# Eight-batch macaron block on one core: the slot-table scatters of the attention stage are issued elsewhere in GpSimd's program

## The reference, cut to what matters

```
x = x + 0.5 * ffn(layernorm(x))      # 8 experts, 2 per token, fixed capacity
x = x + attn(layernorm(x))           # 16 heads, rotary positions, decay mask, no softmax
x = x + 0.5 * ffn(layernorm(x))
```

## Time and profile before

| | us |
|---|---|
| median of 3 runs | 2408.15 |
| the runs | 2403.44, 2408.15, 2408.89 |
| the profiled execution: its own time | 2403.44 |
| its span | 2401.6 |
| PE busy | 2187.6 |
| DVE busy | 1341.5 |
| POOL busy | 1163.4 |
| ACT busy | 1008.5 |

### The profile page before, as it was taken

The page is one execution under the profiler, slowest core; times in us unless marked ns, Lnnn a source line. Parts: engine busy times, 40 slices in busy tenths (PEclk is TensorE's granted clock), DMA queues, the critical chain, the costliest instruction groups (busy, mean ns, idle before and its releaser), DMA issues.

```text
span 2401.6 us, 57464 instructions
## 1 busy us (share of the span) xinstructions
PE 2187.6 (91%) x22468; PEld 1914.7 (80%) x22468; DVE 1341.5 (56%) x3312; ACT 1008.5 (42%) x2149; POOL 1163.4 (48%) x911
## 2 busy tenths in 40 slices
PE   6749999999999996999999999739999999999997
PEld 6738888999999995777777777628888899999997
DVE  7744444555555552577778877645444455555552
ACT  4433334444444441445555555423333343444442
POOL 4754777444444443222244444364776544444443
PEclk9999999999999998999999999859999999999998
DMA  8522433444434334112111211132443434343432
GB/s 331 200 91 48 82 91 84 104 79 98 81 96 92 89 77 98 37 38 73 58 55 57 73 57 74 56 120 49 82 90 78 84 98 84 94 99 82 100 80 29
DMA packets 129221, 209.40 MB, mean 87 GB/s; under 512 B 24876, under 2 KB 105328, under 8 KB 122864
## 3 DMA queue, kind: packets, MB, share of 16 engines
q0 software_dynamic: 57344, 69.21, 17.5%
q1 hardware_dynamic: 71696, 137.62, 16.6%
HBM read 136.03 MB, written 72.88 MB: 87 GB/s over the span
## 4 chain that ended last, share of the span: by engine, by line
PE 50%; DVE 4%; issue 3%; ACT 1%; POOL 1%; another core or an unknown queue 1%; DMA 1%; POOLq 0%; DVEq 0%; ACTq 0%
PE bank L632 15%; PE bank L643 15%; PE bank L716 10%; PE bank L804 3%; PE bank L837 1%; PE bank L772 1%; PE bank L621 1%; PE bank L787 1%; PE bank L822 1%; PE bank L876 1%; PE bank L734 1%; POOL slot_table L381 0%; DVE aw L1756 0%; DVE xnl L1730 0%
## 5 line engine op out<-in xcount | busy, mean ns | idle before, releaser
L1098 ACT ACTIVATE h<-bank 128x512 f32<-128x512 f32 x512 | 307.3, 600 | 923.7 <-PE bank L632 787.2
L1665 DVE CAST hh<-h 128x512 fp32r<-128x512 f32 x512 | 223.9, 437 | 763.6 <-ACT h L1098 683.3
L643 PE MATMUL bank<-w2h,hh 128*128 128x256 f32 x2048 | 585.2, 286 | 5.6 <-issue 5.5
L643 PE MATMUL bank<-w2h,hl 128*128 128x256 f32 x2048 | 582.4, 284 | 4.0 <-issue 3.8
L643 PE MATMUL bank<-w2l,hh 128*128 128x256 f32 x2048 | 582.2, 284 | 4.0 <-issue 3.8
L632 PE MATMUL bank<-xh,w1h 128*128 128x512 f32 x1024 | 411.1, 401 | 12.9 <-issue 6.0
L643 PEld LDWEIGHTS bank<-w2h,hh 128*128 128x128 f32 x2048 | 393.4, 192 | 26.0 <-issue 6.8
L418 POOL DMA_INDIRECT xe<-xn_rows,tab x256 | 272.4, 1064 | 290.7 <-issue 259.8
L643 PEld LDWEIGHTS bank<-w2l,hh 128*128 128x128 f32 x2048 | 393.8, 192 | 23.2 <-issue 6.1
L632 PE MATMUL bank<-xl,w1h 128*128 128x512 f32 x1024 | 408.7, 399 | 1.8 <-issue 1.8
L632 PE MATMUL bank<-xh,w1l 128*128 128x512 f32 x1024 | 402.8, 393 | 1.3 <-issue 1.3
(11 more groups left out here) (209 smaller groups left out, 3312.1 us busy)
## 6 DMA issues: line engine op xcount, KB each, us to landing
stg<-in_L_ffn_w SPq DMA_DIRECT2D x64, 1024.0 KB
xb<-acc SPq DMA_DIRECT2D x9, 1024.0 KB, 8.0
xa<-in_L_attn_x SPq DMA_DIRECT2D x8, 1024.0 KB, 14.0
xn_rows<-xa SPq DMA_DIRECT2D x8, 1024.0 KB
xn_rows<-xn_r SPq DMA_DIRECT2D x8, 1024.0 KB
xr<-acc SPq DMA_DIRECT2D x7, 1024.0 KB
out_rows<-xr SPq DMA_DIRECT2D x7, 1024.0 KB
slot_table<-pay,idx POOLq DMA_INDIRECT x256
```

Source lines behind the costliest of these rows:

```text
L643: last = pe.matmul(o, a[:, fj, s], c[:, fj, :], start=(fj == 0 and n == 0 and t % 2 == 0), stop=(fj == FJ - 1 and n == 2), skip_group_chec ...
L1098: act.activation(h32[fj % 2][:], bank[fj % 2][:], ACT.Gelu_apprx_tanh).then_inc(f.gelu, 1)
L1665: dve.tensor_copy(hh[:, fj, :], h32[fj % 2][:]).then_inc(f.hh, 1)
```

## The change

In POOL's `sequence(b)` the three calls `slots(b - 3, 1)`, `slots(b - 3, 2)` and `slots(b - 3, 3)`, which stood one by one behind `rotated(n + 4)`, `rotated(n + 5)` and `rotated(n + 6)`, are gone. In their place `slots(b - 2, 0)`, `slots(b - 2, 1)` and `slots(b - 2, 2)` stand together behind `rotated(n + 7)`; `slots(b - 2, 3)` takes the place of `slots(b - 2, 0)` behind `residual_power(b - 1)`. All eight scatters of a batch are thus issued in one round, where before two were issued in round b and six in round b+1. In `drain()` the six scatters of batch B-3 are no longer needed.

```
                 rotated(n + 4)
-                slots(b - 3, 1)
                 rotated(n + 5)
                 front_power(b + 1)
-                slots(b - 3, 2)
                 rotated(n + 6)
-                slots(b - 3, 3)
                 rotated(n + 7)
+                slots(b - 2, 0)
+                slots(b - 2, 1)
+                slots(b - 2, 2)
                 rotated(n + 8)
                 residual_power(b - 1)
-                slots(b - 2, 0)
+                slots(b - 2, 3)
                 rotated(n + 9)
             def drain():
                 head_power(B - 1)
-                for j in range(1, NT // 2):
-                    slots(B - 3, j)
                 residual_power(B - 1)
```

## The result

The changed kernel takes 2440.58 us (median of 4 runs, 2436.92 to 2442.09) against 2407.36 us (4 runs, 2403.44 to 2408.89) for the kernel before in the same set of runs: ratio 1.0128, 95% interval 1.0092 to 1.0164. It is 33 us slower, where 2408.5 us was forecast and the range ended at 2413. The profiled execution took 2450.27 us, its span is 2448.5. That is 46.9 us more than the span before, and not all of it is the change's: 16.1 us lie in `ffn(0)`, where nothing was changed, 28.0 in the attention stage, 2.6 in `ffn(1)`.

The account below looks back on a forecast made before the run. The prediction took PE, busy 91% of the span, to bound the kernel. Terms of -1.60 us (old place) and +1.92 us (new place) summed to +0.3 us, giving a 2408.5 us median, range 2402.5 to 2413.

Parts of the forecast that it names:

- Reading of the bound: Whole kernel waits for PE; from `rotated(n+4)` to `rotated(n+8)` PE has practically no gap, and POOL waits for DVE and PE.
- Old place, -1.60 us: Taking six scatters per round from behind `rotated(n+4)` to `rotated(n+6)`, rounds 3 to 7, gains 1.60 us, between 0 and 2.6.
- the excess: Extra time of rounds 3 to 6 over scatter-free round 2, `rotated(n+4)` to `rotated(n+8)`: 1.28 us in all, mean 0.32.
- POOL's time in the new place: Six scatters behind `rotated(n+7)` take 7.7 us, end 7.0 us before `rotated(n+8)`, and are hidden under POOL's idle time.
- New place, +1.92 us: Six scatters behind `rotated(n+7)` cost 0.32 us per round over six rounds, +1.92 us, between 0 and +3.1.
- The pair behind `residual_power` and the drain: Pair keeps place and number, only columns differ: 0; the six scatters removed from the drain kept nobody waiting: 0, at most -0.3.
- Rival A: Slow scatters behind `rotated(n+7)` hold back `rotated(n+8)`; PE 1.6 us late in rounds 2 to 6: +8 us, 2416; chance 0.09.
- The row of 2.58 us: Slowest scatter of round 3, at 1202.71 beside a DVE subtraction with both inputs in SBUF; other scatters about 1 us.
- Rival C: Moved scatters shift stalls of single rounds, as 2.19 us ahead of `turn(n+8)`: -4.3 to +6.4 us; chance 0.20.
- The chances for "slower": Stated probability 0.11 that the whole kernel gets slower by more than about 0.3%, 7.2 us.
- if the part grows by 1 us or more: Sign against the new-place forecast: the window `rotated(n+4)` to `rotated(n+8)`, expected at 36.5 to 37.0 us, growing that much.

Follow-up runs that it names:

- 2340 sets: Sets of runs in which the unchanged kernel took about 2340 us: 2339.19 us in the second set, 2337.27 us in the fourth.
- add_compute: Kernel before plus five small GpSimd `pow`, no DMA, behind `rotated(n+7)` in rounds 2 to 7: 2338.73 against 2339.19 us, ratio 1.0002; repeated as add_compute_b: 2410.76 us, 1.0003.
- third set: Set of runs in which the changed kernel was run again beside the kernel before: 2433.93 against 2409.45 us, ratio 1.0115.
- 2400 sets: Sets of runs in which the unchanged kernel took about 2400 us: 2422.26, 2409.45 and 2425.94 us, and 2407.36 us beside the changed kernel's first result.

## Why the prediction was wrong, by its own steps

- **Reading of the bound: right for the kernel before.** PE has no gaps in the part, and POOL waits for DVE. In the changed kernel POOL still does, but PE is idle 3.73 us of the last 23.59.
- **Old place, -1.60 us: right, and small.** From `rotated(n+4)` to `rotated(n+7)` now takes 19.50 to 19.58 us in all of rounds 2 to 6, where before round 2 took 19.49 and rounds 3 to 6 some 19.7 to 20.0 (36.72 to 37.01 less 17.0): 1.1 us gained over four rounds, forecast 1.28. What the excess is, the prediction did not ask. In the 2340 sets it is absent with the scatters in their old places (add_compute: 19.49 to 19.58 in all five rounds, and `rotated(n+6)` 14.62 to 14.70 behind `rotated(n+4)`). So it comes and goes with the large effect, and was probably its first trace.
- **POOL's time in the new place: right.** Start, duration and end of the scatters are as forecast, and nothing queues behind them. The Trainium skill ("SBUF — State Buffer", Who interferes with whom) was used for the duration, and here it held: 0.97 to 1.09 us each beside masks, residual additions and statistics.
- **New place, +1.92 us, between 0 and +3.1: this step failed.** It stands for all six rounds, and measured 23.59 - 16.98 = 6.6 us in round 2 alone, 5.2 to 7.7 in rounds 2 to 6, 31.6 us over the five for the whole part; the attention stage as a whole is 28.0 us longer (736.3 against 708.3), and 27.3 in the third set (733.7, against 706.4 in add_compute_b). The step took the price of scatters one pair at a time, 0.32 us for three pairs in a round, and multiplied it; in the rounds I read no more than two scatters stood in a row, and the six of the drain stand where PE has little left to do. It asked what the scatters wait for and who waits for POOL. What it had to ask is what other engines lose while POOL issues. The rows for it were in the trace: the first groups of `ffn(1)`, 24.3 to 28.7 us against 23.4 (24.1 to 24.9 in a 2340 set, so what is above that is the effect). I took the attention stage alone.
- **The pair behind `residual_power` and the drain: 0, as forecast** as far as the rows tell.
- **Rival A** had the sign and the place right and the mechanism wrong: no scatter was slow and `rotated(n+8)` follows 13.9 us behind the last. Its price (+8) came from POOL's list. The row of 2.58 us that speaks for it has nine like it in that trace, all beside `ygl`. **Rival C** saw unnamed stalls of about 2 us; I took them for chance. They are not the same effect: the wait ahead of `turn(n+8)` of round 2 stands unchanged in a 2340 set (add_compute, where `turn` is L780):

```profile
1145.20 0.60 PE L780 MATMUL bank<-cst,qk 128*128 128x128 f32 x4 [2.19 <-issue]
```
- **What would prove it wrong:** "if the part grows by 1 us or more" came true, in every round. The chances for "slower" add up to 0.12 (A 0.09, C 0.03) where 0.11 is written; nothing hangs on it.

The same section of the Trainium skill states that DMA doesn't contend with a compute engine and that PE and ACT never wait on anyone. About ports that may be so, no run here shows it; the time of completion is another matter. Beside six indirect DMAs PE's consumers start 4.86 and 3.95 us after the products that they need were recorded as ended, PE waits for ACT in turn (2.55 us before 1169.68), and where the two differ the measurement decides.

**Not settled.** Whether it is PE's signals or PE's last writes that come late: the ffn rows speak for something behind PE's issue, the rows of L840 and the 1.46 us above for its issue too. Whether it would be there without the recording. What decides between a 2400 and a 2340 set: one of each kind ran on the same chip, so it isn't the chip alone. Whether DMAs that another queue issues by index would do it. And whether the changed kernel costs anything in a 2340 set: it never ran in one; the same run of six, added, cost 1.0006 and 1.0008 there.

## What to carry to other kernels

Price a run of indirect GpSimd DMAs by its length as a run, not by the sum of its pieces, and look at what PE's consumers do while it lasts: here two in a row cost next to nothing, six in a row 4.3 to 7.8 us each time, though GpSimd was idle for 14 us behind them, and in a 2340 set nothing. If they may be spread, put them in pairs: with 1.7 us of other work between, three pairs cost 1.2 us. It isn't a rule for every place: two pairs 2.6 us apart cost 3 us and more beside 64 small products of PE. Before an experiment is read, compare the unchanged kernel with its own time in the earlier sets: an effect can be absent from a whole set, and the traces should be checked for missing events.

## What the hardware showed that I had not expected

- In the 2400 sets, runs of four to eight indirect DMAs of GpSimd hold back what waits for TensorE until 1.0 to 1.7 us after the run in rounds 2 to 6 (0.42 in the one group of `ffn(1)` read, where the first 13.5 us of the run held nothing back): in gaps of 17.0 us, +0.4 to 1.2 us for two scatters, +2.6 for four, +4.3 to 7.8 for six, +9.3 to 10.0 for eight. It isn't their data (0.27 of 0.30 MB left out changes nothing), nor GpSimd's being busy (five `pow`: 17.0), nor plain DMAs in a run of 3.40 us (17.0).
- The effect is there in some sets and in others not at all, and the kernel of 2337 us takes 70 to 90 us more in the sets that have it. The traces of those sets miss over a quarter of the semaphore events.
- A stop of PE costs more than its idle time: in round 2 the granted clock was 1.00 up to the end of the stop and 0.86 in the 11.94 us behind it, where the same work took 1.42 us longer. The full rounds have 0.93 to 0.98, against 0.98 to 1.00 before. Another 1.46 us of busy time were lost during the scatters at a clock of 1.00.
